# The last conditioning stage of a four-layer megakernel: from two halves to four quarters, with the small steps moved to GpSimd

## The reference

```
_norm(x)      = sqrt(sum(x*x)).clip(1e-7)
logmap0(x)    = arctanh(clip(n, EPS, 1-1e-5)) * x / n       # n = _norm(x)
expmap0(v)    = tanh(n) * v / n                             # n = _norm(v)
plin(x, w, b) = expmap0(logmap0(x) @ w + b)
ada = t_emb @ w_ada + b_ada;  sh_msa, sc_msa, g_msa, sh_mlp, sc_mlp, g_mlp = split(ada, 6)
xn = layer_norm(logmap0(x));  xm = expmap0(xn * (1 + sc_msa) + sh_msa)
q, k, v = _to_heads(plin(xm, w_q, b_q)), ...                # rescaled per row and per head
attn = softmax(einsum(logmap0(q), logmap0(k)) / 4);  out_h = expmap0(einsum(attn, logmap0(v)))
attn_out = plin(_from_heads(out_h), w_o, b_o)
x = mobius_add(residual, expmap0(g_msa * logmap0(attn_out)))
xm = expmap0(layer_norm(logmap0(x)) * (1 + sc_mlp) + sh_mlp)
ff = plin(plin(xm, w_f1, b_f1), w_f2, b_f2)
return mobius_add(residual, expmap0(g_mlp * logmap0(ff)))
```

## Time and profile before

| | |
|---|---|
| median of 3 runs | 2501.59 us |
| the profiled execution | 2501.92 us, of it span 2500.2 us |
| busy over the span | PE 84%, PEld 68%, DVE 54%, ACT 39%, POOL 10% |
| mean granted TensorE clock | 0.892 |
| this stage | 1849 to 2292 us, 443 us |

### The profile page before, as it was taken

One profiled execution on the slowest core, in us unless ns is written; L12 is line 12 of the kernel. 1 busy time (PEld: TensorE's weight loads), 2 busy tenths in 40 slices (PEclk: granted clock), 3 DMA queues, 4 the chain that ended last, 5 costly groups with the idle time before them and its releaser, 6 DMA issues. The chain is left out here.

```text
span 2500.2 us, 34348 instructions
## 1 busy us (share of the span) xinstructions
PE 2107.1 (84%) x13371; PEld 1693.4 (68%) x13371; DVE 1353.5 (54%) x2579; ACT 985.5 (39%) x1954; POOL 244.1 (10%) x207
## 2 busy tenths in 40 slices
PE   6788689999799999999999883789946777785786
PEld 5477668888687888888888673479934554554554
DVE  2589555777575444444343214456546446454885
ACT  2143255555253444444444220235423344454222
POOL 1144200000000000000000002047710000000000
PEclk7799889999899999999999995689976857897998
DMA  2375221233113121111100000265363001000000
GB/s 77 99 230 159 61 69 58 79 102 101 35 34 78 42 51 34 27 42 34 34 1 1 11 3 0 86 193 131 67 145 93 2 18 34 18 18 35 1 9 26
DMA packets 111492, 146.01 MB, mean 58 GB/s; under 512 B 6661, under 2 KB 94660, under 8 KB 111077
## 3 DMA queue, kind: packets, MB, share of 16 engines
q1 hardware_dynamic: 101220, 129.99, 17.3%
q0 software_dynamic: 10112, 13.85, 3.1%
HBM read 121.83 MB, written 21.99 MB: 58 GB/s over the span
## 5 line engine op out<-in xcount | busy, mean ns | idle before, releaser
L1598 DVE TENSOR_TENSOR m_h_lo<-m_hf,m_h_hi 128x512 fp32r<-128x512 f32 x256 | 172.1, 690 | 359.1 <-ACT m_hf L1573 357.2
L1570 ACT ACTIVATE m_h_hi<-m_h_ps,m_bT 128x512 fp32r<-128x512 f32 x256 | 177.0, 691 | 367.6 <-PE m_h_ps L394 348.0
L1573 ACT ACTIVATE m_hf<-m_h_ps,m_bT 128x512 f32<-128x512 f32 x256 | 175.0, 684 | 0.0
L597 POOL DMA_INDIRECT token_sums<-e_y,slot_row x56 | 145.7, 2602 | 159.4 <-DVE e_y L700 147.2
L662 ACT ACTIVATE e_h_hi<-e_h_ps,e_b1T 128x320 fp32r<-128x320 f32 (+1 forms) x128 | 78.0, 609 | 168.3 <-PE e_h_ps L394 102.2
L1310 DVE TENSOR_TENSOR c_h_lo<-c_hf,c_h_hi 128x512 fp32r<-128x512 f32 x120 | 82.3, 687 | 74.8 <-ACT c_hf L1269 73.7
L716 DVE TENSOR_TENSOR e_h_lo<-e_hf,e_h_hi 128x320 fp32r<-128x320 f32 (+1 forms) x128 | 74.1, 589 | 77.5 <-issue 44.4
L1837 POOL MEMSET n_bias<- 128x256 f32 x1 | 0.3, 312 | 1083.5 <-POOLq L59 1083.5
L1266 ACT ACTIVATE c_h_hi<-c_h_ps,c_b 128x512 fp32r<-128x512 f32 x88 | 62.2, 707 | 109.3 <-PE c_h_ps L394 108.8
L394 PE MATMUL m_y_ps<-m_h_hi,l_w_1hi 128*128 128x512 f32 x256 | 100.3, 392 | 3.5 <-issue 3.5
L394 PE MATMUL m_h_ps<-m_x_hi,l_w_0hi 128*128 128x512 f32 x256 | 100.6, 393 | 0.4 <-ACT m_b2T L1563 0.4
(11 more groups left out here) (644 smaller groups left out, 5607.7 us busy)
## 6 DMA issues: line engine op xcount, KB each, us to landing
cT<-in_L_ffn_W_dram SPq DMA_DIRECT2D x30, 1024.0 KB, 5.3
res<-in_L_cond_ew_dram SPq DMA_DIRECT2D x22, 1024.0 KB, 5.3
cT<-in_L_ffn_w_dram SPq DMA_DIRECT2D x16, 1024.0 KB, 7.0
res<-gates_rows SPq DMA_DIRECT2D x8, 1024.0 KB, 15.0
l_mod<-modulation_rows SPq DMA_DIRECT2D x16, 512.0 KB, 6.6
token_rows<-d_tok SPq DMA_DIRECT2D x2, 2112.0 KB, 9.9
token_sums<-res SPq DMA_DIRECT2D x2, 2048.0 KB, 7.6
res<-token_sums SPq DMA_DIRECT2D x2, 2048.0 KB, 8.4
```

What stands on the lines that cost most here:

```text
L597: pool.indirect_dma_start(out=sums, out_offset=bass.IndirectOffsetOnAxis(ap=st.slot_row[0:r, e, j:j + 1], axis=0), in_=y[0:r, e % 2, j, :] ...
L1570: act.activation(hs[0][:, f, :], h_ps[:, f % HB, :], ACT.Relu, bias=bT[:, at:at + 1])
L1573: act.activation(hf[:, f % HB, :], h_ps[:, f % HB, :], ACT.Relu, bias=bT[:, at:at + 1]).then_inc(act_done, 1)
L1598: dve.tensor_tensor(hs[1][:, f, :], hf[:, f % HB, :], hs[0][:, f, :].bitcast(F32), ALU.subtract).then_inc(h_ready, 1)
```

## The change

`l3_order` is written anew in beats. Each beat from -8 to 47 has at most one tile of qkv, f1 or f2 (`l3_jobs`), some beats wo tiles behind it; beats 0 to 15 have one tile of attention each, with no break between the eighth and the ninth. The chains of small steps are made per quarter (4 tiles) and sit at fixed beats. Quarter q's wo is in beats 4q+6 and 4q+7, its gate in 4q+8, its second norm in 4q+11, its f1 in beats 12+8q to 15+8q, its f2 in the next four.

All chains move to GpSimd (`norm_root`, `norm_chain`, `norm_clip`, `head_chain`, `attn_chain`, `unit_clip`, `gate_root`, `gate_chain`, `hidden_clip`), on 128x4 (12 for three groups, 64 for heads, 192 for heads of q, k, v). A root or a reciprocal is there a `pow` and a Newton step, so ACT keeps only `Ln`, `Tanh` and `Exp`. The stages in program text:

```diff
+def l3_jobs(beat):
+    if beat < 0:
+        return [("qkv", 2 * QUARTERS + beat)]
+    jobs = [("qkv", 2 * QUARTERS + beat)] if beat < 8 else []
+    if 12 <= beat < 44:
+        q, i = (beat - 12) // 8, (beat - 12) % 8
+        jobs.append(("f1" if i < CHUNK else "f2", q * CHUNK + i % CHUNK))
+    for q in range(QUARTERS):
+        i = beat - (q * CHUNK + 6)
+        if i in (0, 1):
+            jobs += [("wo", q * CHUNK + 2 * i), ("wo", q * CHUNK + 2 * i + 1)]
+    return jobs
...
+    def early(beat):
+        for q in range(QUARTERS):
+            k = beat - (q * CHUNK + 4)
+            if k == 4:
+                yield "unit_clip", q
+            if k == 5:
+                yield "gate_root", q
+            if k == 7:
+                yield "norm_log", 2 + q
+                yield "norm_chain", 2 + q
...
+    def late(beat):
+        for q in range(QUARTERS):
+            k = beat - (q * CHUNK + 4)
+            if k == 0:
+                yield "attn_chain", q
+            if k == 1:
+                for t in tiles(q):
+                    yield "attn_scale", t
+            if k == 4:
+                yield from gated(q * CHUNK)
+            if k == 5:
+                yield "tanh", q
+                yield "gate_chain", q
+            if k == 6:
+                for t in tiles(q):
+                    yield "move", t
+                    yield "stats", NT + t
+                yield "norm_root", 2 + q
+            if k == 7:
+                for t in tiles(q):
+                    yield "norm", NT + t
+                yield "norm_clip", QUARTERS + q
...
            def inverse_root(out, a, t):
+                link(pool.tensor_tensor(out, a, power[:, 0:1].to_broadcast([P, width(a)]), ALU.pow))
+                link(mult(t, out, out))
+                link(mult(t, t, a))
+                link(affine(t, t, -0.5, 1.5))
+                link(mult(out, out, t))
+
+            def clip(out, n2, scale=1.0):
+                m, r, t = (k[:, 0:width(n2)] for k in (k1, k2, k3))
+                link(pool.tensor_scalar(m, n2, EPS * EPS, None, ALU.max))
+                inverse_root(r, m, t)
+                return pool.tensor_scalar(out, r, A * scale, scale, ALU.mult, ALU.min)
...
+            def unit_clip(q):
+                last = CHUNK * (q % QUARTERS + 1) - 1
+                pool.wait_ge(squared, square_no["piece", ("wo", last, 0) if q < QUARTERS else ("f2", last, 1)])
+                clip(quarter(fu, q), quarter(nu2, q)).then_inc(unit_ready, 1)
+                pool.wait_ge(unit_ready, q + 1)
...
+            for stage, i in l3_order():
+                if stage in stages:
+                    stages[stage](i)
```

More of the change, by code:

```diff
@@ L1989, in gated @@
     def gated(first):
-        for m in range(first, first + HALF):
+        for m in range(first, first + CHUNK):
             yield "gate", m
@@ L1993, in gated @@
                 yield "dot", m - 1
[L1994 to L2002, removed]
-        yield "stats", n
-    for stage in ("norm_len", "norm_log", "norm_var", "norm_scale"):
-        yield stage, 0
+        yield "dot", first + CHUNK - 1
+    def early(beat):
[9 more added lines that the diff above has]
+        for q in range(QUARTERS):
+            k = beat - (8 * q + 21)
+            if k == 0:
+                yield "unit_clip", QUARTERS + q
+            if k == 1:
+                yield "gate_root", QUARTERS + q
@@ new lines, in late @@
+    def late(beat):
+        for q in range(QUARTERS):
+            k = beat - (q * CHUNK + 4)
+            if k == 0:
+                yield "attn_chain", q
+            if k == 1:
+                for t in tiles(q):
[14 more added lines that the diff above has]
+                yield "norm_clip", QUARTERS + q
+        for q in range(QUARTERS):
+            k = beat - (8 * q + 21)
+            if k == 0:
+                yield from gated(NT + q * CHUNK)
+            if k == 1:
+                yield "tanh", QUARTERS + q
+                yield "gate_chain", QUARTERS + q
+            if k == 2:
+                for t in tiles(q):
+                    yield "move", NT + t
@@ L2006, in l3_order @@
+    for n in range(CHUNK):
+        yield "stats", n
+    yield "norm_root", 0
+    for n in range(CHUNK, NT):
+        yield "stats", n
+    yield "norm_log", 0
+    yield "norm_chain", 0
+    yield "norm_root", 1
     yield "parity", 0
-    for n in range(HALF):
+    for n in range(CHUNK):
         yield "norm", n
-        if n in (2, 3):
-            yield "qkv_turn", n - 2
-    yield "norm_root", 0
+        if n == 1:
+            yield from turn(("qkv", 0), 0)
     yield "norm_clip", 0
[L2014 to L2120, removed]
@@ new lines, in hidden_clip @@
+            def hidden_clip(q):
+                n2 = k5[:, 0:CHUNK]
+                pool.wait_ge(squared, square_no["piece", ("f1", CHUNK * (q + 1) - 1, 1)])
+                link(plus(n2, quarter(nf2[:, 0, :], q), quarter(nf2[:, 1, :], q)))
+                clip(quarter(fac_h, q), n2).then_inc(hid_ready, 1)
+                pool.wait_ge(hid_ready, q + 1)
+            stages = dict(norm_root=norm_root, norm_chain=norm_chain, norm_clip=norm_clip, head_chain=head_chain,
+                          attn_chain=attn_chain, unit_clip=unit_clip, gate_root=gate_root, gate_chain=gate_chain,
+                          hidden_clip=hidden_clip)
@@ L2847, in _ @@
[L2847 to L2851 removed]
+                dve.scalar_tensor_tensor(out=dst[:, t, :], in0=v[:, t, :], scalar=a2[:, t:t + 1], in1=part[:, m % 2, :],
+                                         op0=ALU.mult, op1=ALU.add).then_inc(moved, 1)
@@ L2852, in _ @@
+            stages = dict(stats=stats, norm=norm, piece=piece, qkv_sum=qkv_sum, head_chain=head_chain, head_scale=head_scale,
+                          parity=make_parity, attn_turn=attn_turn, head_sum=head_sum, attn_scale=attn_scale, gate=gate, dot=dot,
+                          move=move)
             for stage, i in l3_order():
```

939 lines of the change are left out of this document (416 added, 523 removed).

## The result

The changed kernel takes 2740.97 us (median of 4 runs, 2737.17 to 2742.09) against 2501.36 for the kernel before on the same chip: a ratio of 1.0957, 95% interval 1.0943 to 1.0971. The forecast was 2481, range 2445 to 2550. It is slower by 240 us, all of it in the last conditioning stage: its last `move` ended at 2291.9 us and ends now at 2531.9.

The account below looks back on a forecast made before the run. The last conditioning stage was taken as bound by waits between engines and the low clock that follows, not TensorE's work. Its stretches plus a 20 us allowance ended it at 2271 instead of 2292: 2501.9 - 21 = 2481 us, range 2445 to 2550.

Parts of the forecast that it names:

- beats 0 to 3: First attention beats of the last conditioning stage: two at low clock, two at high, 38 us, to 1941.
- beats 4 to 7: Attention with four wo tiles, 35 us, plus 6 us of TensorE waiting behind DVE's queue: 41 us, to 1982.
- beats 8 to 23: GpSimd's chains set the pace: 46, 41, 41 and 40 us per four beats, together 168 us, to 2150.
- beats 24 to 43: Twelve f2 tiles at 4.33, eight f1 at 3.9, and 2 for hiccups: 85 us, to 2235.
- tail: Stage end: unit_clip, gates, gate_root, tanh, gate_chain and four moves, 16 us, to 2251.
- allowance: 20 us added for low clock in beats 8 to 23 and colliding engine orders; stage end 2271.
- Entry: Stage start: first scale's chain, eight tiles paced by DVE, then scaling and transposes; first scores at 1903 instead of 1924.3.
- Links: GpSimd chain steps: 0.28 us at 4 columns, 0.41 at 64, 0.67 at 192; a pow taken as an ordinary link.
- GpSimd is dearer: Rival: dearer links, pows and heads in beats 8 to 23; 2538 with all of it, given as 2525; chance 0.28.
- Port sharing: Rival: GpSimd steps wait out DVE's two-operand instructions, 25 us, and DVE loses 7: 2513; chance 0.13.
- The clock did not stay up: Rival denied here: TensorE keeps 2.4 GHz through beats 0 to 23, nothing collides: 2455; chance 0.12.
- No change: Rival: allowance is 40 us instead of 20, early start's gain is given back by beat 23: 2501; chance 0.08.

Follow-up runs that it names:

- f3: Kernel with bit-started wide roots on GpSimd and no narrow Newton steps, plus gate_root first, logarithm and norm_chain later in their beat, attn_scale one beat later: 2492.5 us.

## Why the prediction was wrong, step by step

The step that failed is this one: "No row shows a pow. Below I bound it by an ordinary link, above by that 0.845 us plus the wait, 0.98; I take the ordinary link". The power is 1.05 us at its narrowest, already over that upper bound, and 10.5 and 30.95 where it is wide. Two mistakes are in it. An operation that no row shows was bounded by rows of other operations as if all operations had one price. And it got one bound for all widths, while the same paragraph gave the multiply a price for each of 4, 64 and 192 columns. The sum with the measured price is 2481 + 265 = 2746, where 2741 was measured. That it comes so near is partly luck: without powers the kernel took 12 us more than the sum, and of the powers' 265 us 17 did not reach the end.

The rest by its terms, in us. The third column is the changed kernel, the fourth the one without powers, the last the one without links:

| | forecast | changed | no powers | no links |
|---|---|---|---|---|
| to the first scores | 54 | 101 | 55 | 50 |
| beats 0 to 3 | 38 | 70 | 34 | 32 |
| beats 4 to 7 | 41 | 105 | 49 | 39 |
| beats 8 to 23 | 168 | 285 | 182 | 127 |
| beats 24 to 43 | 85 | 105 | 95 | 83 |
| tail | 16 | 17 | 18 | 10 |
| allowance | 20 | | | |
| sum | 422 | 683 | 433 | 341 |

*Entry.* 1903 was forecast for the first scores; without powers they come at 1903.7, in the changed kernel at 1950.0. TensorE waited 32.9 us for the first head scaling.

*Links.* Right: the narrow links stand 0.28 us apart (0.207 busy), 64 columns 0.40 (0.41 forecast), 192 columns 0.64 (0.67). The Trainium skill (GPSIMD Engine Reference, section 3.1) gives about 2.6 cycles a column for an add with two inputs. At the 1.2 GHz of that section this is 2.2 ns, an estimate; the multiplies here grow by 2.4 ns a column from 4 to 64 columns and by 1.6 from 64 to 192. The page has no price for a power.

*Beats 0 to 3.* Without powers four us too long, and for another reason than a cheaper low beat: the forecast counted two beats low and two high, and no beat was low as a whole. A piece of qkv 5 us after the first scores is still at the low clock (3.62 us at 1908.30), the weighing behind it at the full one (2.04 at 1912.36), and the four beats take 8.7, 7.8, 7.9 and 6.5 us from one row of scores to the next. With powers the second head chain adds a wait of 32.3 us.

*Beats 4 to 7.* The wait that was forecast at 6 us is there, before `head_scale`: 9.6 us without powers, 60.6 with them. TensorE in order of time, in these two kernels:

```profile
1962.92 1.11 PE L2448 MATMUL l_ps<-ident,l_qkv 128*128 128x128 f32 x4 [9.58 <-DVE l_qkv L2651]
```
```profile
2100.39 1.12 PE L2447 MATMUL l_ps<-ident,l_qkv 128*128 128x128 f32 x4 [60.59 <-DVE l_qkv L2650]
```

*Beats 8 to 23.* "Now GpSimd is the pace" holds, by the kernel without links. The size was 182 for 168, and the allowance of 20 took that up. In the changed kernel ACT stood 117 us there for the length that `tanh` needs and 31 for the logarithm's input, and DVE 96 of its 155 us for `attn_chain`. The forecast named these waits behind GpSimd and priced the chains that cause them without their powers.

*Beats 24 to 43.* Ten us short without powers, twenty with them. The waits of over 2 us that should have been absent are two in the changed kernel (3.5 and 2.7 us).

*Rivals.* "GpSimd is dearer" is what happened, and its condition, a power above 0.75 us, was met; its price of 2525, or 2538 with everything, was not, for the same missing widths. Port sharing exists, at 7 us for 254 us of GpSimd multiplies instead of the 32 that were priced. The clock did not stay up: its mean is 0.63 to 0.67 up to beat 23. "No change" was not what came; 2501.2 is what the same order gives with a cheaper root.

*The change's idea.* Of the kernels that compute the reference the best is f3, at 0.9963 (0.9951 to 0.9974): 9 us under the kernel before and 248 under the changed one. The rest of what quarters and unbroken attention could give the links take back: 99 us stand between the no-power kernel and the one without links. Whether a chain with fewer links would keep part of that was not tried.

## What to carry to other kernels

Never give an operation that no trace shows the price of its neighbours: measure it alone, at each width in which the kernel uses it, before anything is built on it. On GpSimd a power costs by the column, some fifty multiplies at 192 columns; start a wide inverse root from the bits, and see whether the result needs the Newton step behind a narrow power at all: here it did not. And when removing a wait moves the time by less than the wait, ask what set it: here three waits on two engines were one queue of chains on a third.

## What the runs showed of the hardware that I had not expected

- A GpSimd power on f32: 1.05, 2.91, 5.42 and 10.55 us at 4, 16, 32 and 64 columns, 30.95 at 192. It was the same on 32 partitions as on 128, for 1.0 and 2.7, and for exponents 1 and -0.5.
- At 4 and 12 columns it is exact enough for this kernel's outputs without a Newton step, and so at 64 and 192 is an integer multiply-add on the bits with two rounds, on DVE and on GpSimd.
- GpSimd and DVE hold each other up only by a little: with 800 multiplies beside it DVE's two-input SBUF instructions grew by up to 0.09 us on average, and the kernel by 0.29%.
- Of a microsecond of GpSimd's time taken out of a chain, 1.0 reached the end in the wide powers, 0.7 in the narrow ones, and 0.65 in the Newton steps.
